# Post-norm decoder, stage of six feed-forward units: order of turned tiles and first projection, and the engine of the rotation adds

## What is computed

```python
def attn_layer(x, Wqkv, qs, ksc, Wo):            # x (4, 256, 128), 16 heads of 64
    q, k, v = split(x @ Wqkv)                      # 128 -> 3 * 1024
    q, k = l2norm(q) * qs, l2norm(k) * ksc
    q = q * cos * scale + rotate_half(q) * sin * scale
    k = k * cos / scale + rotate_half(k) * sin / scale
    sim = q @ k.T * 8, masked to a window of 32 keys and the 32 before
    return softmax(sim) @ v @ Wo
def ffn_layer(x, g, bln, W1, b1, W2, b2):         # 128 -> 2 * 341 -> 128
    a, gate = split(layernorm(x) * g + bln) @ W1 + b1
    return a * gelu(gate) @ W2 + b2
for each of 6 layers:
    x = attn_layer(shift_tokens(x)) + x
    x = ffn_layer(shift_tokens(x)) + x
```

## Time and profile before

| what | us |
|---|---|
| median of three runs | 3172.2 |
| lowest and highest run | 3157.74 and 3173.82 |
| the profiled execution, its own time | 3166.98 |
| its span in the trace | 3165.2 |

### The profile page before, as it was taken

One profiled execution on the slowest core, in us unless ns is written; L12 is line 12 of the kernel. 1 busy time (PEld: TensorE's weight loads), 2 busy tenths in 40 slices (PEclk: granted clock), 3 DMA queues, 4 the chain that ended last, 5 costly groups with the idle time before them and its releaser, 6 DMA issues. The chain is left out here.

```text
span 3165.2 us, 46116 instructions
## 1 busy us (share of the span) xinstructions
PE 2656.3 (84%) x15697; PEld 1564.9 (49%) x15697; DVE 1647.5 (52%) x3712; ACT 1206.0 (38%) x3124; POOL 1128.7 (36%) x956
## 2 busy tenths in 40 slices
PE   5979999658976888888888888888878798699798
PEld 2436776314543555555555555555534544455343
DVE  4445555436635666666666666666445322263333
ACT  1423222003512565556565556565423011145121
POOL 2000000010114978787778787777310000100000
PEclk8989999659957999999999999999978598699799
DMA  2100000000001000000000000000000000000010
GB/s 63 31 1 0 0 0 0 0 7 9 2 1 44 1 21 8 12 18 14 12 11 14 22 8 9 21 8 8 1 14 2 14 27 14 13 9 2 30 31 25
DMA packets 42398, 41.63 MB, mean 13 GB/s; under 512 B 6924, under 2 KB 31283, under 8 KB 42179
## 3 DMA queue, kind: packets, MB, share of 16 engines
q1 hardware_dynamic: 42178, 38.82, 4.7%
HBM read 33.23 MB, written 0.52 MB: 11 GB/s over the span
## 5 line engine op out<-in xcount | busy, mean ns | idle before, releaser
L2980 PE MATMUL ps<-l1fb_wqkv,l1fb_xs 128*128 128x512 f32 x576 | 304.1, 638 | 115.4 <-ACT l1fb_kT L2922 40.0
L2788 POOL TENSOR_TENSOR l1fb_p<-l1fb_p,l1fb_rden 128x640 f32<-128x640 f32 x192 | 240.8, 1254 | 254.3 <-DVE l1fb_rden L2851 254.3
L2846 DVE TENSOR_REDUCE l1fb_shift<-ps 128x4 f32<-128x640 f32 x192 | 158.2, 824 | 326.4 <-PE ps L3010 326.3
L2780 POOL TENSOR_TENSOR l1fb_rinv<-l1fb_ssq,neghalf 128x8 f32<-128x8 f32 x192 | 316.8, 1650 | 0.2
L2936 ACT ACTIVATE l1fb_p<-ps,l1fb_shift 128x128 f32<-128x128 f32 (+1 forms) x768 | 281.2, 385 | 2.0 <-DVE l1fb_shift L2846 1.7
L2778 POOL TENSOR_TENSOR l1fb_qk<-l1fb_qk,l1fb_r 128x512 f32<-128x512 f32 x192 | 243.7, 1269 | 5.0 <-DVE l1fb_r L2837 5.0
L2782 POOL TENSOR_TENSOR l1fb_qk<-l1fb_qk,l1fb_rinv 128x512 f32<-128x512 f32 x192 | 200.7, 1046 | 15.1
L2980 PEld LDWEIGHTS ps<-l1fb_wqkv,l1fb_xs 128*128 128x128 f32 x576 | 96.6, 191 | 207.9 <-issue 57.4
L2943 ACT ACTIVATE l1fb_pT<-ps 128x512 f32<-128x512 f32 x192 | 114.6, 597 | 194.1 <-PE ps L3032 194.1
L2917 ACT ACTIVATE l1fb_sq<-ps 128x512 f32<-128x512 f32 x192 | 114.7, 597 | 186.2 <-PE ps L2980 160.0
L2936 ACT ACTIVATION_READ_ACCUMULATOR l1fb_p<-ps,l1fb_shift 128x1 f32 x768 | 162.7, 212 | 0.0
(11 more groups left out here) (719 smaller groups left out, 5837.0 us busy)
## 6 DMA issues: line engine op xcount, KB each, us to landing
l1fb_wqkv<-in_L_ffn_Wqkv SPq DMA_DIRECT2D x24, 256.0 KB, 2.7
l3f_w<-in_L_ffn_W SPq DMA_DIRECT2D x21, 256.0 KB, 3.0
l2f_w<-in_L_ffn_W SPq DMA_DIRECT2D x16, 256.0 KB, 3.0
l1fb_wqkv<-in_L_ffn_Wqkv SPq DMA_DIRECT2D x6, 512.0 KB, 4.5
l1fb_wo<-in_L_ffn_Wo SPq DMA_DIRECT2D x6, 512.0 KB, 4.0
l1fb_w<-in_L_ffn_W SPq DMA_DIRECT2D x6, 341.0 KB, 2.9
l3x_k<-l3x_k SPq DMA_DIRECT2D x8, 128.0 KB
l1fb_w<-in_L_ffn_W SPq DMA_DIRECT2D x6, 128.0 KB
```

The lines of the kernel that those rows point to most:

```text
L2780: nc.gpsimd.tensor_tensor(w.rinv[:, u, :], w.ssq[:, u, :], chip.neghalf[:, 0:8], ALU.pow).then_inc(*w.unit_norm.end(f"rinv{u}"))
L2788: nc.gpsimd.tensor_tensor(p, p, w.rden[:, c, :, :].rearrange("p j q -> p (j q)").unsqueeze(2).to_broadcast([P, 2 * QT, SEEN]), ALU.mult)\
L2846: nc.vector.tensor_reduce(w.shift[:, c, :, :], ps[:, bank:bank + 2, 0:2 * SEEN].rearrange("p j (q n) -> p j q n", n=SEEN), AX.X, ALU.max, ...
L2980: nc.tensor.matmul(ps[:, PROJ_BANK(u), :], w.xs[:, x.odd, q * P:(q + 1) * P], w.wqkv[:, col:col + 512], start=True, stop=True)\
```

## The change

Three edits, all in this stage.

- **Plans of TensorE and ScalarE.** In `PE_PLAN` each `t` moves to directly behind the `S` of its slot (so `t4'` ahead of `T6'`, `t0` ahead of `T2`, and so on), and `p0` moves from the end of slot 0 into slot 1, behind `T7'`. In `ACT_PLAN` each `e` moves to the front of its slot, ahead of `c` and `X`, and `q0` moves from the end of slot 0 into slot 1, ahead of `X1`. `DVE_PLAN` and `POOL_PLAN` stay.
- **Rotation adds.** For even projections (0, 2, 4, 6) the add of the rotation, 128x512 f32 with both operands in SBUF, leaves GpSimd and is issued by VectorE between the sum of squares and its clamp. For odd ones it stays on GpSimd.
- **Waits.** The even `r` no longer waits for the add two projections back, which is now earlier in VectorE's own list; the new add waits for the products ahead of it on its own engine. The step counts of the two semaphores follow.

```diff
--- before.py
+++ after.py
@@ -2649,12 +2649,12 @@
 
 
 
-PE_PLAN = """S0 T6' gate01' t4' V6' gate2' p0    S1 T7' value01' t5' V7' value2' p1    S2 T0 y2' t6' V0 p2    S3 T1 y1 t7' V1 p3
-             S4 T2 mean t0 V2 p8 p4              S5 T3 var t1 V3 p9 p5                 S6 T4 t2 V4 p10 p6      S7 T5 spread t3 V5 p11 p7""".split()
+PE_PLAN = """S0 t4' T6' gate01' V6' gate2'    S1 t5' T7' p0 value01' V7' value2' p1    S2 t6' T0 y2' V0 p2    S3 t7' T1 y1 V1 p3
+             S4 t0 T2 mean V2 p8 p4           S5 t1 T3 var V3 p9 p5                    S6 t2 T4 V4 p10 p6     S7 t3 T5 spread V5 p11 p7""".split()
 DVE_PLAN = """inv7' att5' max0 edge6' r7' tab    inv0 att6' max1 edge7' g0' g1' r0 g2'  inv1 att7' max2 edge0 x2' r1  inv2 att0 max3 edge1 r2 x1
               inv3 att1 max4 edge2 centre r3     inv4 att2 max5 edge3 vareps r4          inv5 att3 max6 edge4 diag xs r5  inv6 att4 max7 edge5 xn r6""".split()
-ACT_PLAN = """c6' X0 e4' gelu0' gelu1' gelu2' q0    c7' X1 e5' q1    c0 X2 e6' q2    c1 X3 e7' q3
-              c2 X4 e0 v8 q4    c3 X5 e1 v9 q5    c4 X6 e2 v10 q6    c5 X7 e3 v11 q7""".split()
+ACT_PLAN = """e4' c6' X0 gelu0' gelu1' gelu2'    e5' c7' q0 X1 q1    e6' c0 X2 q2    e7' c1 X3 q3
+              e0 c2 X4 v8 q4    e1 c3 X5 v9 q5    e2 c4 X6 v10 q6    e3 c5 X7 v11 q7""".split()
 POOL_PLAN = """s7' n6'    s0 n7'    s1 n0    s2 n1    s3 n2    s4 n3 root    s5 n4    s6 n5""".split()
 
 
@@ -2690,13 +2690,13 @@
         w.feed = Steps(sem("feed"), ["y1", "mean", "var", "spread", "gate01", "value01", "value2", "y2"])
         w.gate2 = Steps(sem("gate2"), ["gate2"])
         w.xsteps = Steps(sem("xsteps"), ["xs"])
-        w.rot = Steps(sem("rot"), [f"{s}{u}" for u in range(QK) for s in ("rot", "ssq", "clamp")])
+        w.rot = Steps(sem("rot"), [f"{s}{u}" for u in range(QK) for s in (("rot", "ssq", "clamp") if u % 2 else ("rot", "ssq", "add", "clamp"))])
         w.max, w.inv = Steps(sem("max"), each("max", ITEMS)), Steps(sem("inv"), each("inv", ITEMS))
         w.edge, w.att = Steps(sem("edge"), each("edge", ITEMS)), Steps(sem("att"), each("att", ITEMS))
         w.norm = Steps(sem("norm"), ["x1", "x1s", "diff", "dsq", "vareps", "diag", "xn0", "xn", "g0", "g1", "g2", "x2"])
         w.sqs, w.turned, w.vals = Steps(sem("sqs"), each("sq", QK)), Steps(sem("turned"), each("e", 8)), Steps(sem("vals"), [f"v{u}" for u in range(8, 12)])
         w.X, w.kept, w.gelu = Steps(sem("X"), each("X", ITEMS)), Steps(sem("kept"), each("c", ITEMS)), Steps(sem("gelu"), each("gelu", 3))
-        w.unit_norm = Steps(sem("unit_norm"), [f"{s}{u}" for u in range(QK) for s in ("add", "rinv", "qk")])
+        w.unit_norm = Steps(sem("unit_norm"), [f"{s}{u}" for u in range(QK) for s in (("add", "rinv", "qk") if u % 2 else ("rinv", "qk"))])
         w.scaled, w.root = Steps(sem("scaled"), each("s", ITEMS)), Steps(sem("root"), ["root"])
         a = chip.a
         block = ctx.enter_context(nc.Block())
@@ -2774,8 +2774,9 @@
     nc.gpsimd.memset(fp(w.p), 0.0).then_inc(w.ready, 1)
 
     def unit_norm(x, u):
-        after(eng, w.rot, f"rot{u}", x)
-        nc.gpsimd.tensor_tensor(w.qk[:, u, :], w.qk[:, u, :], w.r2[:, u % 2, :], ALU.add).then_inc(*w.unit_norm.end(f"add{u}"))
+        if u % 2:
+            after(eng, w.rot, f"rot{u}", x)
+            nc.gpsimd.tensor_tensor(w.qk[:, u, :], w.qk[:, u, :], w.r2[:, 1, :], ALU.add).then_inc(*w.unit_norm.end(f"add{u}"))
         after(eng, w.rot, f"clamp{u}", x)
         nc.gpsimd.tensor_tensor(w.rinv[:, u, :], w.ssq[:, u, :], chip.neghalf[:, 0:8], ALU.pow).then_inc(*w.unit_norm.end(f"rinv{u}"))
         after(eng, w.unit_norm, f"rinv{u}", x)
@@ -2828,7 +2829,8 @@
         k, hh, q = PROJ[u]
         after(eng, w.sqs, f"sq{u}", x)
         after(eng, w.turn, f"t{u // 2 * 2 + 1}", x.past(1))
-        after(eng, w.unit_norm, f"add{(u - 2) % QK}", x.past(0 if u >= 2 else 1))
+        if u % 2:
+            after(eng, w.unit_norm, f"add{(u - 2) % QK}", x.past(0 if u >= 2 else 1))
         src, r1, r2 = heads(ps[:, PROJ_BANK(u), :]), heads(w.qk[:, u, :]), heads(w.r2[:, u % 2, :])
         tab = lambda part, o: w.turn_tab[:, k, part, q, o].unsqueeze(1).to_broadcast([P, 8, o.stop - o.start])
         nc.vector.tensor_tensor(r1, src, tab(0, slice(0, DH)), ALU.mult)
@@ -2837,6 +2839,9 @@
             last = nc.vector.tensor_tensor(r2[:, :, o], src[:, :, other], tab(1, o), ALU.mult)
         last.then_inc(*w.rot.end(f"rot{u}"))
         nc.vector.tensor_reduce(w.ssq[:, u, :], heads(w.sq[:, u % 2, :]), AX.X, ALU.add).then_inc(*w.rot.end(f"ssq{u}"))
+        if u % 2 == 0:
+            after(eng, w.rot, f"rot{u}", x)
+            nc.vector.tensor_tensor(r1, r1, r2, ALU.add).then_inc(*w.rot.end(f"add{u}"))
         after(eng, w.rot, f"ssq{u}", x)
         nc.vector.tensor_scalar(w.ssq[:, u, :], w.ssq[:, u, :], 1e-24, None, ALU.max).then_inc(*w.rot.end(f"clamp{u}"))
 
```

## The result

The changed kernel takes 3075.0 us (median of four runs, 3069.5 to 3080.8) against 3173.0 for the one before: a ratio of 0.9696, 95% interval 0.9653 to 0.9738. The forecast was 3086 in a range from 3056 to 3124. The profiled execution took 3073.55 us, with a span of 3071.8; my figure for it was 3084.

What follows compares the result with a forecast made beforehand. TensorE, waiting only for ScalarE, bounds the stage. Per body 7.8 us goes and 4.5 comes, net 3.3; 20 bodies 66, clock 8, ends 9: 83 off 3166.98 gives 3084, plus 2: 3086 us, range 3056 to 3124.

Steps and rivals of the forecast that it cites:

- (a): TensorE before `p8` to `p11`: four waits of about 0.90 us go, 3.6 us a body.
- (c): TensorE before `gate2'`: the wait for ScalarE's `e` goes, 0.42 us a body with the tail.
- (d): TensorE before `p0`: the wait for a gelu goes, 1.6 us a body with the tail.
- (e): TensorE before `value2'`: the wait for ScalarE's `e` goes, 1.85 us a body with the tail.
- (f): Slots 4 to 7: `V` newly waits for copy `c`, 0.43, 0.43, 0.86 and 0.43, 2.2 us a body.
- (g): Slot 1: `T7'`, sharing bank 5 with `gate2'`, newly waits 0.85 us for the last gelu.
- (h): Behind `S2`: `t6'` newly waits 1.25 us for `att7'`, which VectorE has behind `r0` and `g2'`.
- (i): Behind `S3`: `t7'` newly waits about 0.2 us, as `y2'`, `x2'`, `r1` and `att0` follow each other on VectorE.
- I take 0.63 to the next start: VectorE's new 128x512 add, both operands in SBUF: assumed 0.63 us to the next start, four a body, 2.5 us.
- by the row, which shows no spread, they are not: VectorE's new adds: not held up by GpSimd, since line 2876 takes 424 to 426 ns in all 24 cases.
- 5 x 1.6 us: Ordinary bodies, one in four: the fall of the clock behind slot 0's waits goes, 1.6 us each, 8 us gained.
- More: Rival, 9%: shorter waits also keep the clock up where the loop turns round, half of 18 us, giving 3077.

Runs made afterwards that it cites:

- the adds alone: The kernel before with the even rotation adds on VectorE and both plans as before: 3172.8 us, ratio 1.0000 to the kernel before.
- covered kernels: The changed kernel with `mean`, `y2'` or the like put ahead of `t`, and `c` ahead of `e`, plus variants of it; the first took 3030.6 us, ratio 0.9535.
- other adds: Covered plans with `p0` ahead of `T7'`, VectorE taking the adds of projections 2, 3, 5 and 7 instead of the even ones: 3047.0 us, ratio 0.9601.
- both edits: Covered plans with `p0` ahead of `T7'`, VectorE's adds those of 2, 3, 5, 7, and `g2'` ahead of `r0`: 3018.7 us, ratio 0.9514.
- tiles only: The changed kernel with `p0` and `q0` back at the end of slot 0: 3128.1 us, ratio 0.9866 to the kernel before.
- `p0` only: The kernel before with shared adds and, of the plans, only `p0` and `q0` moved into slot 1: 3140.1 us, ratio 0.9895.
- plans only: The changed kernel with all eight rotation adds back on GpSimd: 3070.1 us, ratio 0.9692 to the kernel before.

## Why the prediction was right

**The terms.** The wait of `p8` to `p11`, of `gate2'`, `p0` and `value2'` all went, as (a), (c), (d) and (e) had it. In their place came (f) with 1.74 us idle in the rows and 2.2 with tails, (g) 0.71 (0.8 with the tail) against 0.85, and (h) 1.07 (1.2) against 1.25; the figures given under (g) and (h) leave 0.8 and 1.19 if one subtracts them, which is nearer still. (i) did not come at all: no wait was seen at `t7'`, where I had 0.2. The body came out at 48.3 against 48.7. Of the 0.4, (i) is half, and the rest are small excesses in steps: a `t` ahead of a `T` costs 0.49, not 0.54, so slots 4 to 7 last 5.69 each, not 5.74.

**The adds.** "I take 0.63 to the next start", (h) rests on it: 0.60 in the rows. That their leaving is worth nothing on GpSimd's side is shown by the adds alone, 1.0000. But "by the row, which shows no spread, they are not" held up was wrong: one add in four is, by 0.9 us. That the time came out right all the same is luck of the place. The held add is the one in slot 5, where the slack was 1.0 us and not the 0.35 of the working (`att3` ends 0.16 ahead of its use with the hold, and would end 0.88 earlier without); in slots 7 and 1, which have next to none, the adds met no product. In the covered kernels one in slot 7 did, and `t4'` waits for it. The Trainium skill's rule, GPSIMD Engine Reference, section Key points, that the two engines contend when a VectorE instruction has two SBUF inputs, agrees with this trace (1.56 instead of 0.68 us). Line 2876's even 424 ns had misled me: in 22 of its 24 cases it ran beside the inverse root, and in two beside nothing. In the new order the same instruction, now line 2881, begins beside a product in 22 of 24 and takes 0.68 to 0.79 us there:

```profile
L2881 DVE TENSOR_TENSOR l1fb_dsq<-l1fb_diff x24: 424/715/785, 1094.5 to 2188.7; 128x256 f32<-128x256 f32 x24
```

**The clock.** 5 x 1.6 us were to come back; six of the sixteen ordinary bodies had been long, and 6 x 1.6 = 9.6 came. That these falls hang on `p0`'s wait is supported from both sides: with it 1.9 us long they come in 14 of 16 ordinary bodies, with `p0` moved alone in one. But that one stands behind the wait of 1.85 before `value2'`, and with other adds two of five stand behind a wait of 1.83 at `t5'`, as in the kernel with both edits. So the clock falls now and then behind a long wait, of 1.5 to 1.9 us here, wherever that stands, and moving `p0` helps by taking one away; "the 1.78 us before `value2'` was not followed by a fall" was true of the trace that I had.

**What was missed.** "What the four bodies where the loop turns round take more [...] I leave as it is": this term I put at nothing, and 6 us came. They took 16 us more than four ordinary ones, 54.4, 57.4, 57.3 and 55.0 (my 18 had the sixth long body in it), and now take 10 more, 50.7, 50.6, 51.4 and 50.6. Windows of two turns before,

```profile
1293.20:1347.57 54.37, 45.06 (x308) 28.26 (x307) 34.04 (x87) 31.44 (x97) 41.64 (x34) 1.00 0.03 8
1505.24:1562.67 57.43, 48.23 (x308) 30.16 (x307) 34.37 (x87) 31.55 (x97) 41.67 (x34) 0.94 0.03 7
```

and of two in the changed kernel:

```profile
1478.46:1529.06 50.60, 44.89 (x308) 28.03 (x310) 37.38 (x91) 31.24 (x97) 37.17 (x30) 1.00 0.03 8
1673.96:1725.39 51.43, 46.46 (x308) 29.23 (x310) 37.59 (x91) 31.43 (x97) 37.17 (x30) 0.97 0.03 8
```

At full clock the turn costs 2.3 us in both kernels, 54.37 against 52.0 and 50.60 against 48.3. What went is the falls of the clock behind it: three of the four turns had them before, five falls in all, and one turn has one now. This is the mechanism of the rival *More*, to which I gave 9%: it brought 6 us and not 9, and the measured median, 3075.0, lies nearer to its 3077 than to my 3086.

Together on the 20 bodies: 20 x 3.7 = 74, clock 9.6, turns 6, which are the 90 us between 1066.1 and 976.1; my sum had 66 + 8 for them. For the ends of the stage I had 9. They brought 7.9 up to the last `x1`, and 4.5 were lost outside it, so that 3.4 are left: 93.4 in the span against my 83.

## What to carry to other kernels

When the copy out of PSUM is late because it stands behind other work of the engine, moving it forward helps only if the work that it waits for, and what waits for it in turn, are moved so that something independent stays between producer and consumer; here 7.8 us a body went away by the working and about half of it came back as waits without cover; putting the cover back gave another 1.7%. Relieving an engine that nobody waits for gained nothing here, though its instructions can still hold those of another. And an add given to VectorE should be placed by what GpSimd runs at that moment, and by whether the engine's next result is late, not by the sum of busy times.

## What the runs showed of the hardware

An f32 VectorE add of 512 columns with both inputs in SBUF that begins while a GpSimd product of 512 columns runs ends about 0.55 us after that product, or after its own 0.68 where that is later; begun at once behind the product's start it takes 1.40 to 1.56 us instead of 0.68. A small clamp with one input (8 columns, 0.17 us) takes 0.97 to 1.01 in the same way, and ends within 0.03 us of the product's end. Beside GpSimd's inverse root of eight columns (1.65 us) the add keeps its 0.68 to 0.69.

Waits of TensorE of 1.83 to 1.90 us were followed by some 3.4 us at the lower of the two clock levels in 14 of 16 ordinary bodies (tiles only, 1.90), in two of five (other adds, 1.83; the same with both edits) and in one of 16 (`p0` only, 1.85). In the kernel before, the wait of 1.49 before `p0` was followed by one in six of 16, and the 1.78 before `value2'` in none. Waits of 1.31 brought none in five (plans only), and those of 0.7 and 1.07 us apart from each other none in 16 (the changed kernel). A turn of the loop cost 2.3 us at full clock in the kernels before and after the change (1.8 in the covered one), and up to 5.4 before where the clock fell behind it.
